# Both halves of a head pair's scores in four PSUM banks, back to back; shared banks emptied by ScalarE, queries' low parts on GpSimd

## The reference

```python
# cross attention, per batch (x is layer-normed twice ahead of it)
q = (lat @ Wq)                      # 256 x 1024, 16 heads of 64
k, v = split(ctx @ Wkv)             # 512 x 1024 each
k = apply_rope(k, cos, sin)
attn = clip(einsum('nd,sd->ns', q, k) * 64**-0.5, -11, 11)   # per head, 256 x 512
x = x + softmax(attn) @ v @ Wo + bo
# second layer
h = rmsnorm(x_ln);  q = h @ Wq + bq;  k, v = split((h @ Wdown + bdown) @ Wup + bup)
att = softmax(einsum('thd,tgd->thg', q, k) / sqrt(8))        # 16 x 16 heads, each token
x1 = x_ln + einsum('thg,tgd->thd', att, v) @ Wo + bo
h2 = rmsnorm(x1);  gate = softmax(h2 @ Wg + bg)              # 8 experts
x = x + x1 + sum_e gate_e * (h2 @ We[e])
```

## Time and profile before

| | |
|---|---|
| median of 3 runs | 307.46 us (307.30 to 307.54) |
| profiled execution | 307.56 us |
| its span, first to last instruction | 305.8 us |
| PE busy | 292.3 us, 96% |
| DVE busy | 246.2 us, 81% |
| POOL busy | 206.7 us, 68% |
| ACT busy | 163.0 us, 53% |

### The profile page before, as it was taken

The page is one execution under the profiler, slowest core; times in us unless marked ns, Lnnn a source line. Parts: engine busy times, 40 slices in busy tenths (PEclk is TensorE's granted clock), DMA queues, the critical chain, the costliest instruction groups (busy, mean ns, idle before and its releaser), DMA issues.

```text
span 305.8 us, 6762 instructions
## 1 busy us (share of the span) xinstructions
PE 292.3 (96%) x2546; PEld 204.8 (67%) x2546; DVE 246.2 (81%) x450; ACT 163.0 (53%) x326; POOL 206.7 (68%) x209
## 2 busy tenths in 40 slices
PE   6999989999999999999999999999999999999983
PEld 6887656766668666666787676556686665577651
DVE  3869999876785869899877798976956699887875
ACT  3656555677444735574426455774436368414532
POOL 7157964666474839686747578599927587978763
PEclk9999999999999999999999999999999999999999
DMA  7623833112110201111201111111101200000001
GB/s 235 170 60 81 216 64 96 36 38 51 45 44 3 51 19 34 38 34 36 55 16 36 35 36 34 27 40 41 36 1 38 51 3 0 2 17 1 2 0 34
DMA packets 15567, 14.24 MB, mean 47 GB/s; under 512 B 3824, under 2 KB 11056, under 8 KB 15536
## 3 DMA queue, kind: packets, MB, share of 16 engines
q1 hardware_dynamic: 15008, 13.49, 17.2%
q10 hardware_dynamic: 528, 0.33, 0.4%
HBM read 4.89 MB, written 0.52 MB: 18 GB/s over the span
## 4 chain that ended last, share of the span: by engine, by line
PE 60%; DVE 17%; POOL 10%; issue 7%; ACT 4%; SPq 1%; DMA 1%; POOLq 0%; DVEq 0%; ACTq 0%
PE sc L670 11%; PE pv L686 11%; PE sums L707 6%; PE pj_k L590 5%; PE side L798 4%; PE pj_k L592 3%; PE pj_k L591 3%; PE side L874 3%; POOL moe L2020 3%; PE pv L885 2%; POOL e L1946 2%; DVE ks L1369 2%; DVE moe L1452 2%; PE side L785 2%; POOL prod L1325 2%
## 5 line engine op out<-in xcount | busy, mean ns | idle before, releaser
L1946 POOL TENSOR_SCALAR e<-e 128x1024 f32<-128x1024 f32 x64 | 70.5, 1101 | 55.9 <-ACT e L995 49.8
L995 ACT ACTIVATE e<-sc 128x1024 f32<-128x1024 f32 x64 | 65.7, 1026 | 33.9 <-PE sc L670 33.6
L670 PEld LDWEIGHTS sc<-qs,ks 64*128 64x128 f32 x768 | 49.6, 185 | 21.6 <-issue 18.3
L670 PE MATMUL sc<-qs,ks 64*128 64x256 f32 x768 | 62.4, 294 | 0.3 <-ACT e L995 0.2
L686 PE MATMUL pv<-e,v 128*64 128x256 f32 x496 | 60.4, 385 | 0.2
L686 PEld LDWEIGHTS pv<-e,v 128*64 128x64 f32 x496 | 32.9, 136 | 20.9 <-issue 4.7
L1939 POOL TENSOR_TENSOR krot<-kcos,kswap 128x512 f32<-128x512 f32 x31 | 42.4, 1367 | 6.6 <-DVE kcos L1442 3.0
L1003 ACT ACTIVATE u<-pv 128x256 f32<-128x256 f32 x31 | 12.0, 386 | 53.0 <-PE pv L686 46.8
L1369 DVE TENSOR_TENSOR ks<-krot,ks 128x512 fp32r<-128x512 f32 x32 | 29.1, 909 | 0.2
L987 ACT ACTIVATE v<-pj_k 128x512 f32<-128x512 f32 x28 | 16.8, 599 | 15.5 <-PE pj_k L592 15.0
L1442 DVE TENSOR_TENSOR ksin<-pj_k,sinT 128x512 f32<-128x512 f32 x32 | 21.9, 684 | 2.5 <-PE pj_k L592 1.8
(11 more groups left out here) (324 smaller groups left out, 577.5 us busy)
## 6 DMA issues: line engine op xcount, KB each, us to landing
kswap<-ksin SPq DMA_DIRECT2D x126, 64.0 KB, 2.0
ctx_in<-in_ctx_dram SPq DMA_DIRECT2D x4, 256.0 KB, 3.7
prod<-in_L_xattn_Wkv_dram SPq DMA_DIRECT2D x2, 512.0 KB, 5.3
prod<-in_L_xattn_Wq_dram SPq DMA_DIRECT2D x1, 512.0 KB, 4.9
wo<-in_L_xattn_Wo_dram SPq DMA_DIRECT2D x1, 512.0 KB, 5.5
fwe<-in_L_ffn_We_dram SPq DMA_DIRECT2D x1, 512.0 KB, 4.2
x_in<-in_x_dram SPq DMA_DIRECT2D x1, 384.0 KB, 5.9
out_dram<-x_in SPq DMA_DIRECT2D x3, 128.0 KB, 1.9
```

The lines of the kernel that those rows point to most:

```text
L670: last = nc.tensor.matmul(sc[:, h, c * NT:(c + 1) * NT], ks[rows, j % 3, k_part, chunk], qs[rows, j % 2, q_part, :], start=(k_part + q_par ...
L995: nc.scalar.activation(e[:, j % 3, :, 2 * half:2 * half + 2, :].rearrange("p h c n -> p h (c n)"), sc[:, :, :], ACT.Exp, scale=SCALE).then ...
L1946: nc.gpsimd.tensor_scalar(a, a, EXP_HIGH, EXP_LOW, ALU.min, ALU.max).then_inc(s_clip, 1)
```

## The change

The scores get four banks: `sc[0]` for half 0 and `sc[1]` for half 1, and PE does both halves one behind the other at the head of a slot. `pj_k` and the rotation of projections go: keys use the bank `pv`, values the first bank of half 1 (`sc[1]`, head 0), queries the second bank of half 0, and `times_values` writes into the first bank of half 0. The exponentials of half 0 are therefore taken head by head, and the first head's instruction lets `times_values` of the pair before start (`s_exp_head`). What stands in a bank of the scores leaves it by ACT: `query_hi` copies the queries twice, the high part and the whole (`q_whole`), and POOL, which gets them from SBUF, makes the low part in place of DVE. Queries run two slots ahead. Side steps have a fourth place d, behind both halves; o_T, norm0 and lat_T go there. On ACT both exponentials come first in a slot, then the split of keys, copies, queries and values; `key_products` stands one slot later in DVE's order, `rotate` behind the clips in POOL's; the second half of `weigh_1` moves to the next slot for all batches. Fillers ahead of the first slots go from 6, 8 and 14 to 4, 4 and 7 (each is two passes).

```diff
+QUERIES_AHEAD = 2
 POST_STEPS = {
-    (1, "a"): "norm0", (1, "b"): "norm1", (1, "c"): "norm2", (2, "a"): "norm3", (2, "b"): "out_proj",
-    (3, "c"): "h_T", (4, "a"): "query_down", (4, "b"): "keyval2", (10, "c"): "o_T", (11, "a"): "out_proj2",
+    (1, "d"): "norm0", (1, "b"): "norm1", (1, "c"): "norm2", (2, "a"): "norm3", (2, "b"): "out_proj",
+    (3, "c"): "h_T", (4, "a"): "query_down", (4, "b"): "keyval2", (11, "d"): "o_T", (11, "a"): "out_proj2",
...
-    "weigh_1a": [(7, 0), (7, 1)],
-    "weigh_1b": [(7, 1), (8, -1)],
+    "weigh_1a": [(7, 1)],
+    "weigh_1b": [(8, -1)],
...
-PREP_STEPS = {(3, "b"): "ctx_T", (6, "a"): "lat_T"}
+PREP_STEPS = {(3, "b"): "ctx_T", (4, "d"): "lat_T"}
-WARM_UP = {"ctx_T": 13, "sin_T": 0, "cos_T": 0, "lat_T": 6, "queries": 8, "scores": 14}
+WARM_UP = {"ctx_T": 13, "sin_T": 0, "cos_T": 0, "lat_T": 4, "queries": 4, "scores": 7}
...
-        sc = es.enter_context(nc.psum_tensor("sc", [128, 2, 512], fp32))
-        sc_bank = [sc[:, h, :] for h in range(2)]
+        sc = [es.enter_context(nc.psum_tensor(f"sc{half}", [128, 2, 512], fp32)) for half in range(2)]
+        sc_bank = [sc[0][:, h, :] for h in range(2)]
+        pj_k = [sc[1][:, h, :] for h in range(2)]
...
             def scores(j, half):
...
-                if j or half:
-                    pe.wait_ge(s_exp, 2 * j + half)
+                    if j:
+                        pe.wait_ge(s_exp, 2 * j - 1)
...
+                    if 2 <= j < NPAIR - 1:
+                        pe.wait_ge(s_u, j - 1)
+                    if 1 <= j < NPAIR - 1:
+                        pe.wait_ge(s_qhi, j + QUERIES_AHEAD)
...
             def times_values(j):
...
+                    pe.wait_ge(s_exp_head, j + 2)
...
+            for slot in range(1, NPAIR - 2):
+                scores(slot, 0)
+                scores(slot, 1)
+                side_at(slot, "d")
+                if PAIRS < slot and slot % 2 == 0:
+                    sums(slot - 1)
+                times_values(slot - 1)
+                if slot <= PAIRS and slot % 2 == 0:
+                    sums(slot - 1)
+                side_at(slot, "a")
+                if slot + QUERIES_AHEAD < NPAIR:
+                    queries(slot + QUERIES_AHEAD)
+                for n in value_units(slot):
+                    values(n, slot)
+                side_at(slot, "b")
                 if slot + KEYS_AHEAD < NPAIR:
...
+                    keys(slot + KEYS_AHEAD)
+                side_at(slot, "c")
...
-                nc.scalar.activation(qs[:, j % 2, 0, :], query_bank(j)[:, 0:NT], ACT.Copy).then_inc(s_qhi, 1)
+                    act.wait_ge(s_qlo, j - 1)
+                nc.scalar.activation(qs[:, j % 2, 0, :], query_bank(j)[:, 0:NT], ACT.Copy)
+                nc.scalar.activation(q_whole[:, j % 2, :], query_bank(j)[:, 0:NT], ACT.Copy).then_inc(s_qhi, 1)
...
+                if half == 0 and j < NPAIR - 2:
+
+                    nc.scalar.activation(dst[:, 0, :], sc[half][:, 0, :], ACT.Exp, scale=SCALE).then_inc(s_exp_head, 1)
+                    nc.scalar.activation(dst[:, 1, :], sc[half][:, 1, :], ACT.Exp, scale=SCALE).then_inc(s_exp, 1)
+                else:
+                    nc.scalar.activation(dst, sc[half][:, :, :], ACT.Exp, scale=SCALE).then_inc(s_exp, 1)
...
+            def query_lo(j):
...
+                nc.gpsimd.tensor_tensor(qs[:, j % 2, 1, :], q_whole[:, j % 2, :], f(qs[:, j % 2, 0, :]), ALU.subtract)\
+                    .then_inc(s_qlo, 1)
```

More of the change, by code:

```diff
@@ L175, in side_order @@
     steps = list(FIRST_STEPS)
[L177 to L180, removed]
+    for slot in range(AFTER):
+        for pos in PLACES:
+            if side_step(slot, pos):
+                steps.append(side_step(slot, pos))
     banks = {(name, b): k for name, b, k in TAIL_STEPS}
@@ L200, in value_units @@
     if slot <= 0:
[L201 to L238, removed]
-    return units
-PROJECTIONS = projections()
-PLACE = {unit: i for i, unit in enumerate(PROJECTIONS)}
+        return []
+    if p >= 5:
+        return [8 * (b + 1) + p - 5] if b + 1 < NB else []
+    return [8 * b + 3 + p] if b < NB and (p or b) else []
 def xattn_ffn(nc, x, ctx, cos, sin, ln_lat_g, ln_lat_b, ln_ctx_g, ln_ctx_b, Wq, Wkv, Wo, bo,
@@ L626, in queries @@
                 cols = slice(128 * p, 128 * p + 128)
+                w_hi, w_lo = (wqS[:, i, cols] for i in range(2))
+                t_hi, t_lo = (latT[:, b % 2, i, :] for i in range(2))
                 if j == 0:
@@ L669, in scores @@
                             rows = slice(DH * h, DH * h + DH)
-                            last = nc.tensor.matmul(sc[:, h, c * NT:(c + 1) * NT], ks[rows, j % 3, k_part, chunk],
+                            last = nc.tensor.matmul(sc[half][:, h, c * NT:(c + 1) * NT], ks[rows, j % 3, k_part, chunk],
                                                     qs[rows, j % 2, q_part, :], start=(k_part + q_part == 0),
@@ new lines, in _ @@
+            keys(0)
+            keys(1)
+            keep_busy(WARM_UP["lat_T"], pv_bank)
+            side_product("lat_T", 0)
+            keys(2)
+            keep_busy(WARM_UP["queries"], pv_bank)
+            queries(0)
+            queries(1)
+            keep_busy(WARM_UP["scores"], pv_bank)
+            scores(0, 0)
+            scores(0, 1)
+            values(0, 0)
+            values(1, 0)
+            queries(2)
+            values(2, 0)
+            keys(KEYS_AHEAD)
+            values(3, 0)
@@ L1225, in _ @@
             for slot in range(1, NPAIR - 2):
-                side_taken(slot - 1, "c")
+                behind = side_step(slot - 1, "c")
+                moe_behind = behind is not None and behind[0].startswith("moe")
+                if not moe_behind:
+                    side_taken(slot - 1, "c")
                 exps(slot, 0)
-                side_taken(slot, "a")
-                query_hi(slot + 1)
+                exps(slot, 1)
+                if moe_behind:
+                    side_taken(slot - 1, "c")
@@ L1230, in _ @@
+                side_taken(slot, "d")
+                key_hi(slot + 1)
                 if slot == 1:
-                    key_hi(2)
                     act.wait_ge(s_spread, 1)
                 attention_copy(slot - 1)
+                second_layer(slot - 1, "end")
                 if side_step(slot, "b") == ("moe0", 0):
                     scale_gates(0)
-                exps(slot, 1)
-                units = value_units(slot)
-                step = side_step(slot, "b")
-                if step and step[0].startswith("moe"):
-                    for n in units[:1]:
-                        value_copy(n)
-                    units = units[1:]
+                side_taken(slot, "a")
@@ L1828, in _ @@
             own(nc.vector.tensor_reduce(odd[:, :], ident.rearrange("p (a two) -> p two a", two=2)[:, 1, :], AX, ALU.add))
-            add_chunks(0, 0)
+            for half in range(2):
+                add_chunks(0, half)
             for slot in range(1, AFTER):
@@ L1870, in _ @@
                 if slot < PAIRS:
-                    add_chunks(slot, 0)
+                    for half in range(2):
+                        add_chunks(slot, half)
             side_taken(AFTER - 1, "c")
@@ L2088, in _ @@
                     clip(slot, 1)
+                if slot + KV_AHEAD < NPAIR:
+                    rotate(slot + KV_AHEAD)
                 second_layer(slot, 1)
-                if b < NB - 1:
+                if 0 <= b < NB - 1:
                     if p == 1:
```

227 lines of the change are left out of this document (97 added, 130 removed).

## The result

The changed kernel takes 309.13 us in the median of five runs (308.95 to 310.92), the kernel before 307.49 beside it (307.30 to 307.57): 1.0061 times as long, with an interval of 1.0046 to 1.0076 (ratios come from the single runs, so they differ a little from that of the medians). I had forecast 299.3, faster.

What follows compares the result with a forecast made beforehand. PE's own stream, busy 96% of the span, was taken as the bound. Terms of -11.9, -1.2, -1.4, +1.8, +3.3, +1.1, +1.2 and -1.1 sum to -8.2: 299.4 us profiled, 299.3 median, range 294.5 to 305.5.

Steps and rivals of the forecast that it cites:

- Point 1: PE's stream in slots 1 to 29: fewer changes of matmul kind save 0.41 us a slot, -11.9 us.
- Point 3: Values unit's wait for DVE's kcos in the loop goes, as values no longer take their bank from keys: -1.4 us.
- point 4: Product with values newly waits for half 0's first-head exponential, 0.11 to 0.14 us in 13 short slots: +1.8 us.
- Point 5: Side steps: less PE work covers the reading of the side bank, 11 steps at 0.3 us each: +3.3 us.
- Point 6: POOL takes the queries' low parts; idle time hides them in an average slot, not in slot 24: +1.1 us.
- Point 8: DVE is full where PE is and nearly keeps pace; half the gain lost in some six slots: +1.2 us.
- point 2: Start: seven fillers fewer ahead of the first scores, with new waits and a keys unit moved into the loop: -1.2 us.
- Point 7: ACT gets 32 copies and split exponentials, 17 us, covered by its idle time: 0.
- Point 9: Tail: the last clip ends 9.7 us behind slot 30's first scores in place of 10.8: -1.1 us.
- The first: Rival: new waits eat most of the gain, ACT or DVE late in most slots, about 304.6 us; chance 17%.
- The slower one: Rival: DVE's keys' low part comes late and holds PE; 318.9 us, or 309 with every second slot held; chance 9%.

Runs made afterwards that it cites:

- whole_exp: The changed kernel with half 0's exponentials in one instruction again instead of head by head: 313.57 us, 1.0184 of the kernel before.
- warm_before: The changed kernel with the earlier 6, 8 and 14 filling matmuls ahead of the first slots in place of 4, 4 and 7: 313.11 us, 1.0176.
- gap: The changed kernel with POOL's low parts of queries between clips and rotation, and weigh_1's second product behind slot 16's and 24's clips and rotation: 310.56 us.

## Why the prediction was wrong

By its own steps, 299.4 for the profiled execution was 9.6 us too low. The start was 0.3 better than forecast, the tail 1.3 worse, and the loop 8.6: points 1, 3 to 6 and 8 add to -5.9, a keys unit of 0.7 that point 2 counts comes on top, and +3.4 was measured. These 8.6 are 2.6 of PE's stream, 4.3 of idle time and 1.7 of half clock.

- **Points 1 and 4** (PE's stream, the product's wait) have the mechanism right, and are a quarter too large. PE's busy time in the loop is 216.85 us where it was 222.00 (the two stretches of the earlier trace rows). Less a keys unit of 0.69 that has come into the loop, and 1.7 us of half clock, that is 7.5 less work where 11.9 - 1.8 = 10.1 was forecast: 2.6 short. Slot 15 and whole_exp show both mechanisms at their sizes. What falls short stands at the keys: from start to start, less the idle time shown, the loop's 28 units take 24.72 us, 0.88 each, where 0.79 was forecast. Between values and scores a unit takes 0.79 (slots 6, 7, 8 and others); beside a side step it takes 0.87 and more (slots 3, 10, 18), part of which is waiting for the side bank. Point 1 had taken these changes of kind as unchanged.
- **Point 2** was -1.2: slot 1 starts 2.17 us earlier, with a keys unit of 0.69 left for later: -1.5. warm_before shows 1.76 us of the start to hang on the fillers.
- **Point 3** is right: no wait of values for kcos is left.
- **Point 5** (side steps, +3.3) is a little too large: by what the intervals between matmuls' starts exceed the usual one of their kind, PE waits some 2.9 us ahead of side steps, 0.8 before (how these were counted leaves some tenths open). **Point 7** (ACT, 0) holds: beyond points 4 and 5 the loop shows no wait for ACT.
- **Points 6 and 8 are the steps that failed.** Point 6 gave POOL 1.1, for slot 24 alone, because its idle time hides the low parts "in an average slot". Measured, clips took 4.4 us of PE's time and a low part 1.0 in slot 3. The wait that slot 24's work makes was foreseen: 1.7 us, in slot 25. Those of slots 3 (1.0 for a clip) and 17 (1.7) were not. The average was the error: the low parts met slots where POOL was already full. Besides, a low part took 0.86 us, not 0.74, and the clips grew from 1.10 to 1.19. These are the groups after, and last the rotation before:

```profile
L1944 POOL TENSOR_SCALAR e<-e 128x1024 f32<-128x1024 f32 x64 | 76.0, 1187 | 7.1 <-ACT e L982 1.9
L1937 POOL TENSOR_TENSOR qs<-q_whole,qs 128x256 fp32r<-128x256 f32 x30 | 25.9, 862 | 0.1
...
L1929 POOL TENSOR_TENSOR krot<-kcos,kswap 128x512 f32<-128x512 f32 x31 | 42.2, 1362 | 22.8 <-issue 18.1
...
L1939 POOL TENSOR_TENSOR krot<-kcos,kswap 128x512 f32<-128x512 f32 x31 | 42.4, 1367 | 6.6 <-DVE kcos L1442 3.0
```

  The clips' idle time ahead, 55.9 us before, is 7.1. New work took 28.4 of it, and 16 us more idle time than before now lies ahead of the rotation, which waits behind the clips for the swapped keys and is too late there to help them. Point 8 priced DVE at 1.2 for keeping pace in six full slots; the keys' low part alone held PE for 2.7, in slots 5, 6 and 14, by the splits of the next batch ahead of it. These stood ahead of it before as well, the tokens' one slot later, in slots of 7.63 and 8.50 us, where they now stand in slots of 6.80 and 6.79, PE's wait included. With the kcos wait gone, and point 4 counted with PE's stream, idle time in the loop was to grow by 4.2 us and grew by 8.5.
- **The half clock** was in no term. In slot 25, with a mean granted clock of 0.83 over 10.17 us, it cost 1.7 us of PE's time; but since slots 25 and 26 are together as long without it (warm_before), POOL would have held PE there anyway. The runs of the changed kernel agree: with a mean clock of 0.999 one took 308.95 us, with 0.990 two took 309.04 and 309.13.
- **Point 9** (tail, -1.1) failed by POOL too: the low part for slot 31 stands behind a product of 2.38 us, and the last clip ends 11.3 us behind slot 30's start, not 9.7. With the low part ahead of the rotation (gap) the rest behind slot 30 is 54.28 us, 0.9 below before.
- **The rivals.** None came as told. The first (waits eat most) had ACT or DVE late in most slots; the long waits came from POOL and DVE, in six slots of the loop, and took more than the end that I had given it. The slower one named DVE's keys' low part, which did hold PE, but in three slots and not by being longer: it took 0.68, 0.69 and 0.68 us ahead of slots 5, 6 and 14, and 0.92 on average where it was 0.91. Its price of 309 is right by accident.

## What to carry to other kernels

Where one engine is the bound at 96%, the next ones at 81% and 68% of the span can still be full in single slots: before a bound is shortened, look at the others slot by slot, and at which work there nobody waits for. A move that removes one stall and brings nothing is no proof against piled-up work, since the next full slot takes its place; moving the work that can wait out of the fullest slots first, and then counting again, brought 2% over the changed kernel here (309.13 to 302.71, all moves together). An engine's idle time covers new work only if it lies where the new work goes.
